# Moving the side work of the eight-head attention phases to other steps

## The chip, the cores and the metric

The kernel runs on one core of a Trainium2 chip. The metric is device time in microseconds (us): the median of three executions, 1615.72 us, with 1610.88 the lowest and 1616.22 the highest. One more execution was profiled; all rows come from it.

## What is computed

Four layers on x of shape (4, 256, 32, 32), float32. Layers 0 and 1 are attention with one head (batch norm, or group norm before it) and aren't touched. Layers 2 and 3 are group norm and attention with 8 heads of 32 channels over 1024 tokens:

```
xn     = groupnorm(x) * w + b                      # 32 groups
q, k, v = split per head of (qkv_w @ xn + qkv_b)
weight = softmax over s of (q_t . k_s) / sqrt(32)  # 1024 x 1024 per head
out    = x_or_xn + proj_w @ (weight @ v) + proj_b  # layer 2 adds xn, layer 3 adds x
```

## The kernel before, in words

The two eight-head layers are computed batch by batch, in groups of four heads: 2 layers x 4 batches x 2 groups = 16 phases, numbered 0 to 15. Every engine runs the same sequence of phases from its own list, and semaphores join them (`all_phases`, L906).

A phase P has 64 steps (`STEPS`). Step s belongs to block J = s // 4 (one tile of 128 keys), head s % 4; steps 0 to 31 are the first half of the queries (h = 0), 32 to 63 the second. In a step TensorE does one score matmul into one of three score banks (L1101) and ScalarE takes its exponential into PR, a ring of four blocks (L1287). Beside this run:

- the weighting of V by the exponentials, eight pieces of one block per half, always two together, at the steps of `WEIGH` (L895); it is TensorE work into psO (L992). `at + 32 * h` is the step; a step past 63 falls into the next phase. Piece 0 of a half waits until VectorE has taken the half before out of psO (`out_done`).
- the sums of the exponentials. GpSimd adds blocks 0 to 5 of a half into PA, five additions (L1328); TensorE multiplies PA and blocks 6 and 7 by ones: the unit "z" (`sums`, L996). VectorE then inverts the sums and scales psO: `take_half` (L1128). The exponentials of a block wait until the ring's slot has been weighted, added or summed: blocks 2 and 10 wait for the sum's reading of block 6, blocks 3 and 11 for the whole z, the others for a weighting and an addition.
- units, TensorE work into one of four banks of psD, in turn, each freed by the engine that takes it; a unit waits until the one four places before it has been taken (`all_taken`, L1012). "a", "m", "e" are 64 tiles of a pass that finds the maxima of the scores, taken by VectorE (L1070, L1152), one per step; "t" and "T" transpose these maxima (L1075), which VectorE negates and SP copies by DMA into a row of the query stacks (L1371) before the next half's scores. "K" and "Q" (two halves each) project the keys and queries of the group after next, taken by ScalarE (L1247, then their rounded "high" part, L1235); GpSimd forms the low part (L1312) and SP copies both into the stacks by 16 DMAs (L1354). "v" are the four value units of the next batch's norm, "p" the four output projections, added to X by VectorE (L1143), "z" the sums.

Odd phases 1 to 13 have K, Q and z only and use `SIDE_AT[0]` (called short here). Even phases 2 to 14 also have v and p and prepare the norm of the next batch (long; `SIDE_AT[1]`). Phase 0 is like a long one without p and with one z, with more tiles (84); phase 15 has no K, Q and only 20 tiles, with p at `LAST_AT`.

The norm in long phases and in phase 0: VectorE's statistics at `BN_AT` (L1189), GpSimd's squares after its third addition and the factors after its fifth (`norm_factors_of`, L115), ScalarE's four passes over the batch at `XN_AT` (two into XH at L1221, two into the unrounded copy at L1223), GpSimd's XL, the rest of it (L1306), in its queue between the additions of the two halves. The first K of a long phase waits for XL (L1040 to L1041). In the short phase, ScalarE waits before it takes the first K until the stack DMAs have read what it will overwrite (L1244 to L1245).

The numbers of a unit are steps: TensorE issues a unit in the first step s with `at <= s`, after that step's score, and the weightings after the units:

```
while todo and todo[0][0] <= s:
    next_unit()
for j, at in WEIGH:
    ...
        if at + HALF_STEPS * h == s:
            weigh(P, p, h, j, place, r)
```

VectorE takes its units and statistics sorted by these same numbers. ScalarE takes a unit one step later, after that step's exponential. GpSimd and SP have no steps: they go through their work in program order as semaphores allow.

Of the kernel before, what the change touches and what calls it, by code (L numbers as in the profile page):

```python
# [38 lines left out]
def attention_stack(nc, x, w0, w1, w2, w3, wp1, wp2, wp3, wv1, par_d, ident_d, gmat_d, out):  # L39
    with ExitStack() as ctx:  # L40
# [51 lines left out]
        def wait(e, s, value):  # L92

            if not isinstance(value, int) or value > 0:
                e.wait_ge(s, value)
# [35 lines left out]
        def single_heads():  # L131

            with ExitStack() as stage:
# [662 lines left out]
                def stack_copies(slot, sides):  # L796
# [17 lines left out]
        LAG = 3  # L814
        ROWS = QUADH * NT // 2

        XN_AT = (31, 34, 35, 36)
        BN_AT = (7.5, 10.5, 15.5, 16.5)

        SIDE_AT = [{"K": (23, 25), "Q": (37.5, 39.5)},  # L820
                   {"v": (6.8, 7.4, 21, 22.5), "K": (47, 49), "Q": (55, 57.5), "p": (15, 39, 16, 23.5)}]
        Z_AT = (37, 6)
        FIRST_AT = {"k": (0.1, 0.2), "q": (0.3, 0.4), "b": (1,), "K": (28.1, 30.1), "Q": (32.1, 34.1)}
        W3_AT = 28
        LAST_AT = {"p": (43.5, 47.5)}
# [4 lines left out]
        def side_units(g, first=False, last=False):  # L830
# [8 lines left out]
            else:  # L839
                halves, step = dict(LAST_AT if last else SIDE_AT[g]), STEPS / max(len(tiles), 4 * ROWS)  # L840
                halves["z"] = Z_AT
                if first:
# [49 lines left out]

        WEIGH = [(0, 10), (1, 10), (2, 19), (3, 19), (4, 28), (5, 28), (6, 33), (7, 33)]  # L895
        PIECES = NT - 1

        def weighed(P, J):
# [30 lines left out]
        def eight_heads_in(stage):  # L929
# [48 lines left out]
            with nc.Block() as block:  # L978
                @block.tensor
                def _(e):  # L980
# [103 lines left out]
                    def phase(P, p, G, g, place, r, layers, proj=None, norm=None, norm_b=None):  # L1084
                        todo = [(at, k) for k, (_, at, _) in enumerate(UNITS[place])]

                        def next_unit():
                            unit(place, r, todo.pop(0)[1], P, p, G, g, norm, layers)
# [7 lines left out]
                        for s in range(STEPS):  # L1096
# [7 lines left out]
# [3 lines that stand above are left out]
                                if at + HALF_STEPS - STEPS == s and not (isinstance(P, int) and P == 0):  # L1107
# [5 lines left out]
                    def tail():  # L1113
                        for j, at in WEIGH:
                            if at + HALF_STEPS >= STEPS:
                                weigh(NGRP - 1, 1, 1, j)
                        e.wait_ge(vec_free, TAIL["vector"] + AFTER - BANKS + 1)
                        sums(bank(4, AFTER), NGRP - 1, 1, LAST_ADDS).then_inc(d_full, 1)
                        for c in range(CT):
                            e.wait_ge(vec_free, TAIL["vector"] + AFTER + c - BANKS + 2)  # L1120
                            output(bank(4, AFTER + 1 + c), 2 * c + 1, 2 * NGRP, 3).then_inc(d_full, 1)
# [5 lines left out]
                def _(e):  # L1127
# [46 lines left out]
                    def phase(P, p, G, g, place, r, layers, proj=None, norm=None, norm_b=None):  # L1174
                        events = [(at, 0, k, "unit") for k, (u, at, i) in enumerate(UNITS[place])
                                  if u not in "vkqKQ"]
                        if norm is not None and P is not None:
                            events += [(at, 0, k, "stats") for k, at in enumerate(BN_AT)]
                        if P is None:
# [27 lines left out]
                def _(e):  # L1207
                    def input_ready(place, r, G, norm, layers):
                        e.wait_ge(factors_done, norm + 1)
                        if place:  # L1210
                            used = [x[::2] for x in UNITS[place]].index(("v", NT // 2 - 1)) + 1
                            e.wait_ge(d_full, base_of("all", place, r) + used)
                            if layers[2] == 3:
                                stacks_filled(e, G)
# [35 lines left out]
                    def phase(P, p, G, g, place, r, layers, proj=None, norm=None, norm_b=None):  # L1250
# [9 lines left out]
                        if norm is not None and P is not None:  # L1260
                            events += [(at, 0, "x", i) for i, at in enumerate(XN_AT)]
                        if layers[0] != layers[1]:
# [7 lines left out]
                        for s in range(STEPS):  # L1270
                            J = s // QUADH
                            if s % QUADH == 0:
# [9 lines left out]
                                else:  # L1282
                                    wait(e, sum_done, ADDS * 2 * P - max(ADDS - 4 - J, 0))
                            if norm is not None and s == XN_AT[0]:
                                input_ready(place, r, G, norm, layers)
# [176 lines left out]
```

## Time and profile before

| | |
|---|---|
| median of three executions | 1615.72 us |
| the profiled execution's own time | 1611.06 us |
| its span | 1609.3 us |
| mean granted TensorE clock | 0.977 of full |
| TensorE, weight loads, VectorE, ScalarE, GpSimd busy | 96%, 61%, 65%, 54%, 61% |
| the 16 eight-head phases | from 549.4 us to the end |

A timeline row reads: start in us from the span's start, duration, engine, line, operation, what it writes from what it reads, shapes, and xN for N merged instructions; in brackets the engine's idle time before it and what ended that. Matmuls are pipelined: a row's duration is longer than the distance to the next start, so distances between starts tell what the engine can do. A row by windows gives, for a stretch, the length, each engine's busy time with the number of instructions of the row's form, the granted clock as a share of full, the share of DMA time and GB/s.

### The profile page before, as it was taken

What the parts mean: (1) busy time and instruction counts of PE and PEld (TensorE: products, weight loads), DVE (VectorE), ACT (ScalarE), POOL (GpSimd) and SP (SyncE); (2) the same over time, 40 slices, a digit from 0 to 9 for tenths busy, and PEclk for the clock granted to TensorE, in tenths of its full rate; (3) what the DMA queues carried; (4) which work ended last, traced back from release to release, by engine and by line L of the source; (5) the groups of instructions that cost most, each with busy time, mean ns of one, the idle gap of its engine ahead of it and who ended that gap; (6) DMA issues with size and microseconds to landing.
All of it is one profiled execution on the core that took longest, in us unless ns stands there. A gap on an engine that the chain in (4) does not pass through costs nothing.

```text
span 1609.3 us, 21730 instructions
## 1 busy us (share of the span) xinstructions
PE 1538.1 (96%) x8246; PEld 987.4 (61%) x8246; DVE 1039.3 (65%) x1658; ACT 866.3 (54%) x1440; POOL 974.5 (61%) x388
## 2 busy tenths in 40 slices
PE   5899979999999899999999999999999999999998
PEld 2777868888887555555555556555555556555542
DVE  3666655454553677777776776777777677777651
ACT  3544414343433366656657657656665665756663
POOL 1222302221213288788798698977878879869883
PEclk7999989999999799999999999999999999999999
DMA  5000000000001503031230330303303123042000
GB/s 190 1 20 20 1 1 1 0 1 0 20 1 40 118 14 79 1 79 34 46 79 1 79 72 28 79 12 69 80 1 80 30 76 79 1 106 65 15 27 27
DMA packets 36392, 67.53 MB, mean 42 GB/s; under 512 B 5760, under 2 KB 7872, under 8 KB 36288
## 3 DMA queue, kind: packets, MB, share of 16 engines
q1 hardware_dynamic: 36144, 65.74, 16.9%
q8 instruction: 66, 1.08, 0.3%
q10 hardware_dynamic: 144, 0.39, 0.1%
q14 instruction: 38, 0.31, 0.1%
HBM read 8.15 MB, written 4.19 MB: 8 GB/s over the span
## 4 chain that ended last, share of the span: by engine, by line
PE 60%; POOL 3%; DVE 3%; issue 1%; SPq 1%; ACT 1%; DMA 0%; DVEq 0%; ACTq 0%; POOLq 0%
PE psO L992 14%; PE psD L1070 13%; PE psD L89 12%; PE psA L1101 10%; PE psD L1004 5%; PE psO L1101 5%; POOL PA L1328 3%; DVE BNS L1152 1%; PE psD L1065 1%; SPq L1362 0%; DVE sums_turned L1131 0%; ACT PR L1287 0%; DVE A L1135 0%; DVE A L1137 0%; POOL KQ L1312 0%
## 5 line engine op out<-in xcount | busy, mean ns | idle before, releaser
L1152 DVE TENSOR_REDUCE BNS<-psD 128x1 f32<-128x512 f32 x1024 | 638.6, 681 | 207.1 <-PE psD L1070 201.7
L1328 POOL TENSOR_TENSOR PA<-PA,PR 128x2048 f32<-128x2048 f32 x126 | 578.5, 4592 | 33.4 <-ACT PR L1287 18.6
L1287 ACT ACTIVATE PR<-psA 128x512 f32<-128x512 f32 x688 | 392.3, 603 | 226.2 <-PE psA L1101 203.4
L1070 PE MATMUL psD<-STK 96*128 96x512 f32 x1016 | 409.0, 407 | 3.8 <-ACT KQ L1247 1.9
L1101 PE MATMUL psA<-STK 97*128 97x512 f32 x688 | 290.1, 424 | 3.9 <-DMA STK<-MROW 2.3
L1287 ACT ACTIVATE PR<-psO 128x512 f32<-128x512 f32 x336 | 202.3, 602 | 159.8 <-PE psO L1101 159.6
L705 POOL TENSOR_SCALAR P<-P,RS 128x1024 f32<-128x1024 f32 x64 | 72.0, 1125 | 330.6 <-DVE RS L413 330.6
L992 PE MATMUL psO<-PR,V 128*32 128x512 f32 x2048 | 246.6, 598 | 5.8 <-DVE A L1137 5.6
L1070 PEld LDWEIGHTS psD<-STK 96*128 96x128 f32 x1016 | 195.5, 193 | 56.1 <-DVE BNS L1152 15.9
L1328 POOL TENSOR_TENSOR PA<-PR 128x2048 f32<-128x2048 f32 x32 | 146.8, 4587 | 99.9 <-ACT PR L1287 99.9
L1101 PEld LDWEIGHTS psA<-STK 97*128 97x128 f32 x688 | 130.4, 190 | 111.1 <-issue 58.0
L1101 PE MATMUL psO<-STK 97*128 97x512 f32 x336 | 146.8, 437 | 1.7 <-DMA STK<-MROW 1.1
L992 PEld LDWEIGHTS psO<-PR,V 128*32 128x32 f32 x2048 | 53.2, 109 | 127.4 <-issue 81.4
L645 ACT ACTIVATE PTH<-psA 128x1024 fp32r<-128x1024 f32 x64 | 65.5, 1024 | 105.0 <-PE psA L301 105.0
L1101 PEld LDWEIGHTS psO<-STK 97*128 97x128 f32 x336 | 63.7, 190 | 84.1 <-issue 46.3
L638 ACT ACTIVATE P<-psD,NM 128x1024 f32<-128x1024 f32 x64 | 71.2, 1113 | 79.3 <-DVE NM L406 78.9
L406 DVE TENSOR_REDUCE NM<-psD 128x1 f32<-128x1024 f32 x64 | 77.8, 1217 | 55.2 <-PE psD L89 54.9
L419 DVE TENSOR_TENSOR PTL<-psA,PTH 128x1024 fp32r<-128x1024 f32 x64 | 78.2, 1221 | 44.9 <-ACT PTH L645 44.9
L316 PE MATMUL psO<-PTH,VH 128*128 128x512 f32 x256 | 105.1, 411 | 0.0
L1312 POOL TENSOR_TENSOR KQ<-KQ 128x1024 fp32r<-128x1024 f32 x32 | 75.8, 2392 | 42.4 <-ACT KQ L1235 42.4
L316 PE MATMUL psO<-PTH,VL 128*128 128x512 f32 x256 | 100.4, 392 | 0.0
L316 PE MATMUL psO<-PTL,VH 128*128 128x512 f32 x256 | 100.0, 391 | 0.0
(159 smaller groups left out, 1951.8 us busy)
## 6 DMA issues: line engine op xcount, KB each, us to landing
STK<-KQ SPq DMA_DIRECT2D x128, 256.0 KB, 3.8
STK<-KQ SPq DMA_DIRECT2D x128, 128.0 KB, 3.7
X<-x SPq DMA_DIRECT2D x4, 1024.0 KB, 7.3
out<-X SPq DMA_DIRECT2D x3, 1024.0 KB, 6.4
XN<-w SPq DMA_DIRECT2D x2, 768.0 KB, 6.5
KH<-KL SPq DMA_DIRECT2D x8, 128.0 KB, 2.8
QH<-KL SPq DMA_DIRECT2D x6, 128.0 KB, 2.4
KQ<-w SPq DMA_DIRECT2D x1, 768.0 KB, 4.3
```

Of the source, the lines that this page charges most:

```text
L89: last = e.matmul(out_ap, w, m, start=(i == 0), stop=(i == len(terms) - 1))
L316: mm = e.matmul(psO[:, t, :], vv[:, s, cols], pp[:, h, s, :], start=(s == k == 0), stop=(s == NT - 1 and k == 2))
L406: e.tensor_reduce(NM[:, g % 4:g % 4 + 1], psD[:, index[u] % 2, :], AX.X, ALU.max, negate=True).then_inc(max_done, 1)
L419: e.tensor_tensor(PTL[:, i // 4, :, cols], psT.rearrange("p (s t) -> p s t", s=NT), PTH[:, i // 4, :, cols].bitcast(F32), ALU.subtract).th ...
L992: mm = e.matmul(psO[cols, 0, :], V[:, j, PART * p + CH * q:PART * p + CH * q + CH], source[:, q, :], start=(j == 0), stop=(j == NT - 1))
L1004: mm = e.matmul(full[CH * q:CH * q + CH, :], ones[:, 0:CH], source[:, q, :], start=(j == NT), stop=(j == NT - 1))
L1070: mm = e.matmul(full, QS[0:STACK, group, int(u in "ae"), q, tile * PART:(tile + 1) * PART], KS[0:STACK, group, h, q, :], start=True, stop= ...
L1101: e.matmul(score_bank(s, p), KS[0:STACK + 1, p, j // (NT // 2), q, j % (NT // 2) * PART:(j % (NT // 2) + 1) * PART], QS[0:STACK + 1, p, h, ...
L1152: top = e.tensor_reduce(MXH[:, h, q, tile:tile + 1], full, AX.X, ALU.max)
L1287: e.activation(PR[:, J % 4, (s % QUADH) * HALF:(s % QUADH + 1) * HALF], score_bank(s, p), ACT.Exp, scale=scale).then_inc(exp_done, 1)
L1312: e.tensor_tensor(low_part(which).bitcast(F32R), low_part(which), high_part(which), ALU.subtract).then_inc(low_done, 1)
L1328: e.tensor_tensor(PA[:, :], PR[:, (J - 1) % 4, :] if j == 1 else PA[:, :], PR[:, J % 4, :], ALU.add).then_inc(sum_done, 1)
```

## The change

Only the step numbers move; no instruction is added or removed, and GpSimd's and SP's programs are as before.

```diff
-        XN_AT = (31, 34, 35, 36)
-        BN_AT = (7.5, 10.5, 15.5, 16.5)
-
-        SIDE_AT = [{"K": (23, 25), "Q": (37.5, 39.5)},
-                   {"v": (6.8, 7.4, 21, 22.5), "K": (47, 49), "Q": (55, 57.5), "p": (15, 39, 16, 23.5)}]
-        Z_AT = (37, 6)
+        XN_AT = (32, 37, 38, 38)
+        BN_AT = (3.5, 12.5, 14.5, 15.5)
+
+        SIDE_AT = [{"K": (25.9, 41.7), "Q": (42.6, 58.2)},
+                   {"v": (9.1, 10.6, 11.9, 24.9), "K": (42.4, 44.5), "Q": (45.5, 50.8), "p": (25.2, 17.2, 26.4, 39.6)}]
+        Z_AT = (41.0, 9.0)
...
-        WEIGH = [(0, 10), (1, 10), (2, 19), (3, 19), (4, 28), (5, 28), (6, 33), (7, 33)]
+        WEIGH = [(0, 15), (1, 15), (2, 21), (3, 21), (4, 29), (5, 29), (6, 35), (7, 35)]
```

`Z_AT` holds the step of z for the first half of the own phase ("z0", 37 to 41) and for the second half of the phase before ("z1", 6 to 9).

## Rows read from the trace of the kernel before

**Rows 1.** The page, busy time and share of each engine:

```profile
PE 1538.1 (96%) x8246; PEld 987.4 (61%) x8246; DVE 1039.3 (65%) x1658; ACT 866.3 (54%) x1440; POOL 974.5 (61%) x388
```

**Rows 2.** Busy time by windows: phases 0, 7, 9, 10 and 15:

```profile
core 0: us, PE busy (x) PEld busy (x) DVE busy (x) ACT busy (x) POOL busy (x), PEclk, DMA share, GB/s
549.43:619.74 70.31, 66.51 (x354) 40.35 (x355) 51.76 (x89) 44.82 (x78) 54.49 (x23) 0.98 0.21 46
...
1012.10:1072.61 60.51, 58.64 (x332) 32.30 (x330) 45.02 (x77) 37.85 (x72) 49.13 (x12) 1.00 0.24 53
...
1144.22:1203.37 59.15, 58.40 (x332) 32.39 (x330) 45.01 (x77) 37.85 (x72) 45.78 (x12) 1.00 0.24 54
1203.37:1274.96 71.59, 71.47 (x398) 41.98 (x399) 50.48 (x88) 44.69 (x78) 62.34 (x26) 1.00 0.20 45
```

**Rows 3.** Timeline of TensorE, the last tiles of phase 9, first score of 10:

```profile
1202.42 0.40 PE L1070 MATMUL psD<-STK 96*128 96x512 f32 x1
...
1202.88 0.39 PE L1070 MATMUL psD<-STK 96*128 96x512 f32 x1
1203.37 0.47 PE L1101 MATMUL psA<-STK 97*128 97x512 f32 x1
```

**Rows 4.** Timeline of TensorE in phase 9: z1, what follows, weighting 0/1:

```profile
1149.63 1.06 PE L1004 MATMUL psD<-PA,ones 128*32 128x512 f32 x8
...
1152.35 0.50 PE L1101 MATMUL psO<-STK 97*128 97x512 f32 x1
1152.69 0.40 PE L1070 MATMUL psD<-STK 96*128 96x512 f32 x1
...
1155.15 1.92 PE L992 MATMUL psO<-PR,V 128*32 128x512 f32 x16 [0.66 <-DVE A L1137]
```

**Rows 5.** Timeline of VectorE behind the same z1:

```profile
1152.48 0.72 DVE L1131 STREAM_TRANSPOSE sums_turned<-psD 128x512 f32<-128x512 f32 x1 [1.54 <-PE psD L1004]
...
1155.01 2.48 DVE L1152 TENSOR_REDUCE BNS<-psD 128x1 f32<-128x512 f32 x4
```

**Rows 6.** Timeline of TensorE in phase 0: score 32, fifth tile behind z0:

```profile
583.01 0.50 PE L1101 MATMUL psO<-STK 97*128 97x512 f32 x1 [1.13 <-DMA STK<-MROW]
...
595.02 0.50 PE L1070 MATMUL psD<-STK 96*128 96x512 f32 x1 [1.35 <-DVE BNS L1152]
```

**Rows 7.** Timeline of ScalarE in phase 10: norm passes two to four:

```profile
1245.10 1.23 ACT L1223 ACTIVATE KQ<-X,SC 128x1024 f32<-128x1024 f32 x1
...
1246.70 1.24 ACT L1221 ACTIVATE XH<-X,SC 128x1024 fp32r<-128x1024 f32 x1
...
1248.31 1.24 ACT L1223 ACTIVATE KQ<-X,SC 128x1024 f32<-128x1024 f32 x1
```

**Rows 8.** Timeline of GpSimd in phase 10: the second XL:

```profile
1249.70 2.37 POOL L1306 TENSOR_TENSOR XL<-KQ,XH 128x1024 fp32r<-128x1024 f32 x1 [0.84 <-ACT KQ L1223]
```

**Rows 9.** Timeline of TensorE in phase 10: an output unit:

```profile
1249.90 1.88 PE L89 MATMUL psD<-A,WP 128*128 128x512 f32 x4
```

**Rows 10.** Timeline of GpSimd: additions of a second half, phases 9 and 10:

```profile
1184.84 4.60 POOL L1328 TENSOR_TENSOR PA<-PR 128x2048 f32<-128x2048 f32 x1 [7.77 <-ACT PR L1287]
...
1256.76 18.85 POOL L1328 TENSOR_TENSOR PA<-PA,PR 128x2048 f32<-128x2048 f32 x4
```

**Rows 11.** Timeline of ScalarE in phase 7: taking the first K:

```profile
1037.87 0.69 ACT L1247 ACTIVATE KQ<-psD,PAR 128x512 f32<-128x512 f32 x1 [1.99 <-DMA STK<-KQ]
```

**Rows 12.** Timeline of TensorE in phase 7, behind that:

```profile
1038.61 0.50 PE L1070 MATMUL psD<-STK 96*128 96x512 f32 x1 [1.11 <-ACT KQ L1247]
```

**Rows 13.** Timeline of TensorE in phase 15: z0:

```profile
1569.31 1.07 PE L1004 MATMUL psD<-PA,ones 128*32 128x512 f32 x8 [2.18 <-POOL PA L1328]
1570.17 3.24 PE L1004 MATMUL psD<-PR,ones 128*32 128x512 f32 x16
```

**Rows 14.** Timeline of GpSimd in phase 15: its first addition:

```profile
1545.78 4.57 POOL L1328 TENSOR_TENSOR PA<-PR 128x2048 f32<-128x2048 f32 x1 [4.04 <-ACT PR L1287]
```

**Rows 15.** Busy time by windows in phase 15, columns as in rows 2:

```profile
1572.00:1574.00 2.00, 2.00 (x10) 0.57 (x3) 0.55 (x1) 0.00 (x0) 0.00 (x0) 0.50 0.00 0
```

## The prediction

> **What bounds the kernel now.** I read the page's busy shares first. TensorE shows 96% [rows 1], but matmuls overlap, so the share alone proves nothing. I then cut the span into its 16 eight-head phases [rows 2]. Phases 1, 3, ... 13 (short) take 59.1 us, phases 2, 4, ... 14 (long, with values, output and the next batch's norm) 71.6 us, each kind the same to 0.1 us, but for phase 7 with 60.5. A phase has 64 steps; a step is one score matmul, one maxima tile and whatever the lists place there.
>
> Next the timeline of TensorE, by starts. A tile follows the last tile after 0.46 to 0.47 us [rows 3], two instructions with no wait between. A sum ("z") holds the stream from 1149.63 to 1152.35, 2.72 us [rows 4]. I added such start-to-start costs over both lists of units: about 57.7 us for a short phase, 70.7 for a long one. So TensorE's own stream is the bound, and true waits are some 1.4 us of a short phase and 0.9 of a long one. The change removes no instruction: all it can win is these waits, 7 x (1.4 + 0.9) = 16 us, and those of phases 0, 7 and 15. What it can lose is new waits at the new places.
>
> The short phase's waits: block 0 of the weighting (step 10) needs the half of the output that VectorE frees after z1; TensorE idles 0.66 us before it [rows 4], 0.73 with the restart. The first score of the next phase comes 0.49 us after the last tile, where 0.24 is usual, as the row of maxima lands late [rows 3]. Some 0.4 us lie behind the two transposes of maxima. In the long phase z1 waits about 0.2 us for GpSimd's last addition; the rest is crumbs.
>
> **The change, part by part.** All in us of one phase.
>
> *z1 from step 6 to 9, weighting 0/1 from 10 to 15 (short phases, and 15).* VectorE starts on a sum 2.85 after the sum's first matmul (1152.48 - 1149.63) and begins its next maxima reduction 5.38 after it; reductions end every 0.6, the first 0.68 after its start [rows 4, 5]. So the first tile behind a sum is read 6.06 to 6.11 after the sum began. Units share four PSUM banks in turn. Before, four tiles (steps 7 to 10) stand between sum and weighting; now six do (10 to 15). The fifth needs the bank of the first: it would be issued 3.06 + 4 x 0.47 = 4.94 after the sum's start [rows 4] and may at 6.11, a wait of 1.17; the next tile loses 0.1 more. This wait is in the trace already: in phase 0, where five tiles follow z0, the fifth idles 1.35 us for the reduction [rows 6]. The weighting then comes later than the 5.5 it needs [rows 4] and waits no more. So 0.73 is removed and 1.27 put in its place: +0.54. Bounds: -0.73 if the banks come free in time, +1.1 if one more reduction stands before; I take the value that rows 6 are nearest to.
>
> The Trainium skill, "Perfetto Trace Analysis", section Optimization Strategy, says that a gap repeating on the engine that should be saturated can mean too little PSUM for the next tile. By it the sign here is a loss, where the removed wait alone would make -0.73 x 8 = -5.8; the trace's 1.35 us agrees with the page.
>
> *Row of maxima, transposes.* The second transpose keeps step 54, but a query unit and both later weightings now lie behind it, 7.7 before the phase's end instead of 6.6, so the 0.24 at the border goes [rows 3]; no key or query stands right behind a transpose any more, -0.2. On SP's queue nothing new stands before that row. Short phase in sum: +0.54 - 0.24 - 0.2 = +0.1; seven give **+0.7** (bounds -6 to +4).
>
> *Long phases.* z1 at step 9 finds GpSimd done: -0.2. Behind z1 three value units separate the tiles, so the bank wait does not come. z0 moves from 37 to 41 with keys and queries at 43 to 46 behind it; the second key half needs the bank of the first tile and loses some 0.25. Crumbs behind transposes and before weighting 8 go, -0.45. Output units and batch-norm statistics (VectorE, steps 3.5 to 15.5) cost the same elsewhere: VectorE is free behind the value units. Sum -0.4; seven give **-2.8** (bounds -5.6 to +3.5).
>
> *Keys five steps sooner, norm passes later.* The first key unit waits on GpSimd's low parts XL. ScalarE's four passes go to steps 32, 37, 38, 38. A pass starts 1.6 after the last when an exponential stands between, at most its own 1.24 when none does [rows 7]; GpSimd's second XL starts 0.15 after the last pass and takes 2.37 [rows 7, 8]. From score 37 that is 0.46 + 0.5 + 1.6 + 2 x 1.24 + 0.15 + 2.37 = 7.55. TensorE comes to the key after 6 x 0.47, an output unit of about 1.75 (four matmuls, 1.88 with their tail [rows 9]), a sum with its restart 2.9 and a score 0.23: 7.7. Cost zero, with a margin of 0.15 only. Bounds 0 and 2 per long phase. In phase 0 no output unit stands between: +1.2 there.
>
> *GpSimd and SP behind it.* Five additions take 4.60 + 18.85 [rows 10]. In the short phase z0 now comes before both queries and one key half, so the second chain starts 36.7 into the phase, not 40.6 [rows 10]; in the long one it starts 0.6 later, behind XL, and ends 1.8 us into the next phase, before exponential 4 asks for it at 4.4. Two low parts and the 16 stack transfers on SP follow; the keys' eviction in the short phase waits for these, and itself moves from step 24 to 27. In phase 7 that wait is 1.99 us on ScalarE [rows 11] and 1.11 on TensorE [rows 12]; three steps later, with a weighting behind it, it is covered: **-1.4** (60.5 - 59.1; bounds -1.4 to 0).
>
> *Exponentials.* Blocks 2 and 10 reuse a buffer that the sum must have read: step 8 now waits for z1 at 9, step 40 for z0 at 41. About 2 us on ScalarE, hidden since no score needs those exponentials until the sum is over (three score banks). If that cover failed it would cost 2 per half.
>
> *Phase 15.* No maxima tiles after step 20; GpSimd's additions end the waits: z0 idles 2.18 us [rows 13], and the granted clock is 0.50 of full behind it, the lower of its levels [rows 15]. GpSimd's chain starts 9.35 into the phase [rows 14], now about 0.95 after z1's start at 6.8, 1.6 sooner; and z0 at 41 lets steps 38 to 41 run first. About 3.3 saved, +0.54 as above: **-2.8** (bounds -4.5 to 0).
>
> *Phase 0.* Score 32 waits 1.13 us for its row of maxima [rows 6]; a weighting now lies between: gone. The 1.35 shrinks to 0.25. Query 0 no longer blocks a bank near its end (-1). Against that the key's +1.2, and some 0.8 more in longer runs of tiles. Net **-1.5** (bounds -4 to +2).
>
> Sum: +0.7 - 2.8 - 1.4 - 2.8 - 1.5 = **-7.8 us**, against the profiled execution's own 1611.06 (span 1609.3): 1603.3. The three runs shown are 1610.88, 1615.72 and 1616.22; with the profiled one they lie at two levels 5 us apart, so the same sum on the median 1615.72 is 1607.9. I state the middle, **1606**. A measurement of this kernel can tell about 0.3%, 5 us, from no change.
>
> **Rivals.** Times from 1611.06.
> 1. *Nothing measurable.* New waits eat the gain: the bank wait is 1.8 instead of 1.27 in eight phases (+4.2) and phase 0 wins nothing (+1.5): -2.1 in all, 1609. For: three of the gains are read from one phase each. Against: rows 6 fix the bank wait's size. Chance 0.20.
> 2. *Slower.* The key unit of the long phases waits on XL. Place: step 43, behind ScalarE's norm passes; margin 0.15. It decides from 1.8 us late: 7 x 1.8 = 12.6 turns -7.8 into +4.8. At 2.5 late it is +9.7, 1621. For: if exponential 37 lags, the passes and XL lag with it. Against: exponential 37 follows a weighting, where ScalarE has just caught up. Chance 0.08.
> 3. *The clock falls* behind the new 1.2 us idle. Sixteen matmuls of a sum take 3.24 us at the lower level [rows 13], at full clock some 2.72 x 16/24 = 1.8 [rows 4]: 1.4 x 7 = 10 lost, +2, 1613, no change. Against: short phases keep 1.00 with an idle of 0.66, and phase 0, with its 1.35, has 0.98 over all [rows 2]. Chance 0.04.
>
> A page speaks for rival 3: the Trainium skill, "TensorE: Matmul & The Clock Gate", section A second HAM failure mode: psum-queue depth-cycling, where small idles between groups that cycle through banks let the clock swing. The trace has the fall in phase 15 alone.
>
> **How the numbers follow.** The forecast has 0.68, the rivals 0.20, 0.08 and 0.04. The range 1596 to 1616 holds the forecast at both levels, part of the better bounds (-13 on the lower level) and rival 1. Faster by over 0.3%: 0.68; within: 0.20 + 0.04 = 0.24; slower: 0.08.
>
> **What would show it.** Right: short phases at 59.0 to 59.4 us with an idle of 1.1 to 1.3 us at the tile of step 14, released by VectorE, and none before weighting 0; long phases near 71.2 with the key at 43 unhindered; phase 7 no longer apart; phase 15 near 70. Wrong: an idle before the key units released by GpSimd; short phases under 58.5 (no bank wait) or over 60; a granted clock under 1.00 in short phases.

## The result and the profile after

The changed kernel takes 1618.15 us (median of 15 executions, 1614.22 to 1620.25), the kernel before 1613.5 beside it (15 executions, 1610.88 to 1617.14): a ratio on record of 1.0031 (the two medians alone give 1.0029), 95% interval 1.0022 to 1.0039. It is slower by 0.3%, 4.65 us, and 2.15 us above the top of the forecast range. The two profiled executions, spans 1617.7 and 1609.3, differ by 8.4. Of that, 1.6 lie ahead of the eight-head stage, in code that the change does not touch; over thirteen profiled kernels that code took between 546.8 and 551.7 us, so these 1.6 are not the change's. Another 1.7 are the clock's at the very end of phase 15, which came out differently in these two profiles (last section); 5.1 are left, near the 4.65 of the medians. The 6.8 us of the eight-head stage, these 1.7 included, have their places:

| us | before | after | difference | forecast |
|---|---|---|---|---|
| phase 0 | 70.31 | 67.58 | -2.7 | -1.5 |
| phases 1, 3, 5, 9, 11, 13, each (phase 3 after: 60.09) | 59.15 | 59.86 | +0.7 | +0.1 |
| phase 7 | 60.51 | 59.85 | -0.7 | -1.3 |
| phases 2, 4, 8, 10, 12, 14, each | 71.61 | 71.45 | -0.15 | -0.4 |
| phase 6 | 71.68 | 76.08 | **+4.4** | -0.4 |
| phase 15 | 72.83 | 75.08 | +2.2 | -2.8 |

Against the forecast of -7.8, these +6.8 are 14.6 too much: phase 15 has 5.0 of them, phase 6 4.8, the seven short phases 4.6, the other long ones 1.4; phase 0 is 1.2 better. The extra 0.2 of phase 3 came back in every profile of the changed lists and was not followed up.

By windows, phases 6 and 15 of the kernel before (columns as in [rows 2]):

```profile
940.42:1012.10 71.68, 71.52 (x398) 41.96 (x399) 50.50 (x88) 46.02 (x80) 62.45 (x27) 1.00 0.23 56
```

```profile
1536.43:1609.26 72.83, 62.00 (x334) 24.69 (x332) 23.88 (x40) 33.63 (x66) 41.81 (x11) 0.97 0.04 15
```

and of the changed kernel, phases 0, 6, 7, 9, 10 and 15:

```profile
550.99:618.58 67.59, 66.28 (x355) 40.38 (x356) 51.89 (x90) 45.24 (x78) 52.61 (x22) 0.97 0.21 48
941.25:1017.33 76.08, 72.86 (x398) 42.99 (x399) 50.79 (x88) 46.35 (x80) 61.62 (x26) 0.98 0.22 53
1017.33:1077.18 59.85, 58.74 (x331) 32.49 (x330) 45.02 (x77) 38.26 (x72) 49.92 (x13) 1.00 0.24 54
1148.63:1208.49 59.86, 58.75 (x331) 32.49 (x330) 45.00 (x77) 38.26 (x72) 51.11 (x13) 1.00 0.24 54
1208.49:1279.94 71.45, 71.45 (x398) 41.79 (x399) 50.62 (x88) 44.99 (x78) 57.09 (x25) 1.00 0.20 45
1542.58:1617.66 75.08, 64.27 (x334) 25.20 (x332) 23.76 (x40) 33.62 (x66) 42.72 (x11) 0.95 0.04 15
```

A phase whose length differs from its like is where to look first: phase 6 stands 4.6 us over phase 10, with the same list of units. Its TensorE timeline stops at step 43:

```profile
990.08 0.50 PE L1101 MATMUL psA<-STK 97*128 97x512 f32 x1
990.41 0.40 PE L1070 MATMUL psD<-STK 96*128 96x512 f32 x1
990.65 0.39 PE L1101 MATMUL psA<-STK 97*128 97x512 f32 x1
994.26 0.70 PE L89 MATMUL psD<-XH,WH 128*128 128x512 f32 x2 [3.22 <-POOL WL L1337]
```

and GpSimd's, in the same stretch:

```profile
976.13 0.20 POOL L129 TENSOR_TENSOR SC<-PAR,TMP 128x2 f32<-128x2 f32 x1
985.61 2.38 POOL L1306 TENSOR_TENSOR XL<-KQ,XH 128x1024 fp32r<-128x1024 f32 x1 [9.27 <-ACT KQ L1223]
988.35 2.38 POOL L1306 TENSOR_TENSOR XL<-KQ,XH 128x1024 fp32r<-128x1024 f32 x1 [0.36 <-ACT KQ L1223]
990.69 3.43 POOL L1337 TENSOR_TENSOR WL<-KQ,WH 128x1536 fp32r<-128x1536 f32 x1
```

Phase 6 is where the weights change from layer 2 to layer 3. The key unit needs the low part of the new weights, WL, which GpSimd takes behind both XL. XL was ready in time (988.35 + 2.38 = 990.73), as forecast; WL ends at 994.12. Before, the key came at step 47, at 994.66, after WL's end at 992.57, and nothing waited:

```profile
989.09 3.48 POOL L1337 TENSOR_TENSOR WL<-KQ,WH 128x1536 fp32r<-128x1536 f32 x1
```

In the short phases, TensorE of phase 9 behind z1 (the rows that answer to [rows 4]):

```profile
1155.45 1.06 PE L1004 MATMUL psD<-PA,ones 128*32 128x512 f32 x8
...
1160.15 0.39 PE L1101 MATMUL psA<-STK 97*128 97x512 f32 x1
1161.57 0.51 PE L1070 MATMUL psD<-STK 96*128 96x512 f32 x1 [1.03 <-DVE BNS L1152]
1161.91 0.40 PE L1101 MATMUL psA<-STK 97*128 97x512 f32 x1
1162.16 0.49 PE L1070 MATMUL psD<-STK 96*128 96x512 f32 x1
1162.59 1.92 PE L992 MATMUL psO<-PR,V 128*32 128x512 f32 x16
```

The fifth tile starts 6.12 after z1 (1161.57 - 1155.45), when VectorE has read the first; the weighting waits no more. Both are the forecast's. The page on which the prediction leaned here, the Trainium skill's "Perfetto Trace Analysis", section Optimization Strategy (a gap that repeats on the engine that should be saturated can mean too little PSUM for the next tile), agrees with this trace: the gap of 1.03 stands in every short phase.

In phase 15, TensorE from z0 on:

```profile
1577.11 1.90 PE L1004 MATMUL psD<-PR,ones 128*32 128x512 f32 x16
1578.94 0.50 PE L1101 MATMUL psA<-STK 97*128 97x512 f32 x1
1579.28 0.40 PE L1101 MATMUL psO<-STK 97*128 97x512 f32 x1
1579.51 0.39 PE L1101 MATMUL psA<-STK 97*128 97x512 f32 x1
1581.80 3.16 PE L89 MATMUL psD<-A,WP 128*128 128x512 f32 x4 [1.90 <-issue]
1583.97 1.42 PE L1101 MATMUL psA<-STK 97*128 97x512 f32 x1
```

TensorE reaches score 42 2.5 us sooner, but the output unit p0, left at 43.5, now has three scores between itself and z0 instead of seven. It needs the half that VectorE takes after z0 (`take_half`), and TensorE idles 1.90. The profile calls this idle "issue" and names no releaser; VectorE's last operation on that half ends at 1581.70, and p0 starts at 1581.80:

```profile
1581.01 0.69 DVE L1137 TENSOR_TENSOR A<-psO,A 128x512 f32<-128x512 f32 x1
```

### The profile page after: what moved, and what is told of

Its sections match the earlier page's. It is cut to its first block, busy times and chain, and to the rows that moved or that the text cites. A ratio compares the mean times of both kernels' runs of the same rounds, so it can differ in the third digit from the quotient of the medians.

```text
span 1617.7 us, 21730 instructions
## 1 busy us (share of the span) xinstructions
PE 1547.0 (96%) x8246; PEld 990.7 (61%) x8246; DVE 1040.1 (64%) x1658; ACT 871.8 (54%) x1440; POOL 974.6 (60%) x388
## 4 chain that ended last, share of the span: by engine, by line
PE 64%; DVE 2%; ACT 1%; issue 1%; POOL 1%; DVEq 0%; DMA 0%; ACTq 0%; POOLq 0%
PE psO L992 15%; PE psD L1070 14%; PE psD L89 12%; PE psA L1101 11%; PE psD L1004 5%; PE psO L1101 5%; PE psD L1065 1%; DVE BNS L1152 1%; DVE sums_turned L1131 0%; DVE A L1135 0%; DVE A L1137 0%; ACT PR L1287 0%; POOL PA L1328 0%; PE psD L1075 0%; POOL WL L1337 0%
## 5 line engine op out<-in xcount | busy, mean ns | idle before, releaser
L1070 PE MATMUL psD<-STK 96*128 96x512 f32 x1016 | 416.3, 415 | 8.7 <-DVE BNS L1152 8.7
L1101 PE MATMUL psO<-STK 97*128 97x512 f32 x336 | 143.4, 427 | 0.9 <-ACT PR L1287 0.8
```

Of the source, the lines that this page charges most:

```text
L1070: mm = e.matmul(full, QS[0:STACK, group, int(u in "ae"), q, tile * PART:(tile + 1) * PART], KS[0:STACK, group, h, q, :], start=True, stop= ...
L1101: e.matmul(score_bank(s, p), KS[0:STACK + 1, p, j // (NT // 2), q, j % (NT // 2) * PART:(j % (NT // 2) + 1) * PART], QS[0:STACK + 1, p, h, ...
```

## The experiments

Each is the changed kernel with one edit, unless said. Lengths of phases repeat to about 0.1 us from run to run (phase 15 excepted). Where only one time is given, it is that of the profiled execution, and the reading goes by the lengths of phases, not by that total.

**Keys and queries of the long phases back.**

```diff
-"K": (42.4, 44.5), "Q": (45.5, 50.8)
+"K": (47, 49), "Q": (55, 57.5)
```

> The changed kernel with the keys and queries of the long phases back at steps 47, 49 and 55, 57.5; all else as changed. Theory A (the early key waits for the split of layer 3's weights, once, in phase 6): phase 6 falls from 76.1 us to 71.4 to 71.8, its first key starts without an idle, the other phases stay within 0.2 us, short ones at 59.85. Rival B (phase 6 is longer because GpSimd's additions and XL come later after the moved sum): phase 6 stays above 74 us. Time about 4.5 us under the changed kernel by A, no change by B.

Measured: one time of 1631.84. Phase 6 took 73.58, as the other long phases: its extra is gone, so it does hang on the key's place. But every long phase went from 71.45 to 73.58, and phase 0 from 67.58 to 71.92. With tiles instead of keys behind z0, the fifth meets the bank again: 1.3 of the 2.1, with the restart. Another 0.6 stands at the weighting at 61; what it waits for was not followed. TensorE in phase 10 of this run:

```profile
1265.45 0.39 PE L1101 MATMUL psA<-STK 97*128 97x512 f32 x1
1266.89 0.50 PE L1070 MATMUL psD<-STK 96*128 96x512 f32 x1 [1.04 <-DVE BNS L1152]
```

So the key's new place pays for much of the sum's: these two moves belong together.

**Phase 15's output units later.**

```diff
-LAST_AT = {"p": (43.5, 47.5)}
+LAST_AT = {"p": (47.5, 51.5)}
```

> The changed kernel with phase 15's two output units four steps later (47.5 and 51.5), so as far behind the moved sum as before; all else as changed. Theory A (the first output unit waits there for VectorE's half of the output, and the TensorE clock falls behind the idle): the idle of 1.90 us is gone, the output unit takes about 1.9 us and not 3.16, and phase 15 up to its last score shortens by 2.5 to 3.5 us from 56.99. Rival B (phase 15 is longer because of its other moved steps, the weighting pieces or GpSimd): less than 1 us.

Measured: 1615.55; phase 15 72.24 instead of 75.08, the rest unchanged. z0 (3.14 and 3.15) and the end behind score 63 (18.09 in both) took the same time in the two profiles, so the 2.84 are p0's: its wait, and the slow matmuls behind the wait. TensorE goes from score 44 to score 45, where p0's wait stood, in 0.62:

```profile
1578.44 0.40 PE L1101 MATMUL psA<-STK 97*128 97x512 f32 x1
1579.06 0.49 PE L1101 MATMUL psA<-STK 97*128 97x512 f32 x1 [0.22 <-ACT PR L1287]
```

**Weighting blocks 0 and 1 sooner, everywhere.**

```diff
-WEIGH = [(0, 15), (1, 15), ...
+WEIGH = [(0, 13), (1, 13), ...
```

> The changed kernel with weighting pieces 0 and 1 at step 13 instead of 15; all else as changed. Theory A (the wait is for a PSUM bank at the fifth tile behind a sum): with four tiles between sum and weighting the tile at step 14 waits no more, the weighting idles 0.6 to 0.9 us for VectorE instead, and short phases fall from 59.85 to 59.1 to 59.4 us. Rival B (VectorE's work behind the sum has to be waited for in any order): the wait of the weighting is as long as the tile's was, 1.3 us, and short phases stay at 59.7 to 60. Long phases within 0.2 us by both.

Measured: 1625.05. The short phases fell to 59.00, as theory A has it, but the long ones rose to 73.24 and phase 0 to 70.98, which neither theory had. There the weighting at 45 no longer covers the time in which ScalarE takes the key and query units; TensorE in phase 10 of this run:

```profile
1270.26 0.51 PE L1070 MATMUL psD<-STK 96*128 96x512 f32 x1 [0.34 <-ACT KQ L1247]
1270.61 0.40 PE L1101 MATMUL psO<-STK 97*128 97x512 f32 x1
1270.85 0.40 PE L1070 MATMUL psD<-STK 96*128 96x512 f32 x1
1271.89 0.50 PE L1101 MATMUL psA<-STK 97*128 97x512 f32 x1 [0.64 <-ACT PR L1287]
```

**These three at once.**

> The three edits together (keys and queries of the long phases back, phase 15's output later, weighting 0/1 at step 13), the rest as changed. By theory A of the three: 4.5 + 3 + 7 x 0.6 = 11 to 12 us under the changed kernel, so about 1606 to 1607 where the changed kernel has 1618, and 6 to 8 us under the kernel before (0.4 to 0.5%). By the rivals: no faster than the kernel before.

Measured: 1621.96 (seven executions) against 1612.63 (twelve), ratio on record 1.0044 (1.0058 by the medians), interval 1.0024 to 1.0063. A miss: phase 6 was cured (73.21), but the long phases stood at 72.80 and phase 0 at 71.79. Repairs that each undo a part of the change for all phases take away its gains too; the next ones touch one phase type each.

**Blocks 0 and 1 sooner in the short phases alone.**

```diff
 for j, at in WEIGH:
+    at -= 2 * (j < 2 and place == 2)
```

> The changed kernel, with blocks 0 and 1 of the weighting at steps 13 and 45 in phases 1, 3, ... 13 alone; the long phases keep 15 and 47. Theory A (the loss of the short phases is the fifth tile's bank, behind a sum, in front of a weighting that came too late; what the run with 13 everywhere lost, it lost in the long phases, where the weighting at 47 covers ScalarE's keys and queries): short phases 58.9 to 59.0 us instead of 59.85, long phases 71.45 as in the changed kernel, phase 6 76.1, phase 15 75.1; the span 6 us below the changed kernel's at equal length before the eight-head phases. Rival B (the 0.9 us of the short phases in that run were paid for by work pushed over the border, so that the long phases lose the 1.8 whatever their own steps are): long phases 73.2 again. Rival C (run to run): short phases at 59.85.

Measured: 1611.12. Short phases 59.00, long 71.52, phase 6 76.15: theory A. In the first half step 13 takes 3.16, with the weighting's old wait in it, as step 10 did before, and steps 14 and 15 wait no more; in the second half step 45 takes 2.42 where step 47 took 2.62.

**The low part of the weights first.**

```diff
 factors(norm, place, r, layers[2])
-input_low(norm, norm_b, layers[2])
 if layers[0] != layers[1]:
     e.wait_ge(w3_high, 1)
     e.tensor_tensor(WL[:, :, :], ...).then_inc(w3_split, 1)
+input_low(norm, norm_b, layers[2])
```

> The changed kernel, with GpSimd taking the low parts of layer 3's weights (3.4 us) before the low parts of the input in phase 6, instead of after them. Theory A (phase 6 lost 4.4 us because its first key unit, now at step 43, waits for the low parts of the weights, which stood in GpSimd's queue behind those of the input; GpSimd idles 9 us ahead of these): phase 6 at 71.4 to 71.8 us instead of 76.08, the key at step 43 with a wait under 0.5 us, every other phase as in the changed kernel. Rival B (ScalarE's rounding of the weights in phase 6 makes the norm passes late, and the split is only what ends last): phase 6 stays over 73, the key waiting for the low parts of the input instead. Rival C (GpSimd's port or memory conflicts with the exponentials' additions): the additions lengthen, phase 6 over 74.

Measured: 1617.19; phase 6 71.53, every other phase but the last within 0.1. GpSimd in phase 6, WL now in the stretch in which it had idled, and TensorE's key behind it:

```profile
978.07 3.50 POOL L1336 TENSOR_TENSOR WL<-KQ,WH 128x1536 fp32r<-128x1536 f32 x1 [1.14 <-ACT WH L1228]
986.24 2.38 POOL L1306 TENSOR_TENSOR XL<-KQ,XH 128x1024 fp32r<-128x1024 f32 x1 [4.67 <-ACT KQ L1223]
988.98 2.38 POOL L1306 TENSOR_TENSOR XL<-KQ,XH 128x1024 fp32r<-128x1024 f32 x1 [0.36 <-ACT KQ L1223]
```

```profile
991.27 0.39 PE L1101 MATMUL psA<-STK 97*128 97x512 f32 x1
991.62 0.70 PE L89 MATMUL psD<-XH,WH 128*128 128x512 f32 x2
```

Theory A again: 4.5 us of the result were this one order. Phase 15 took 76.63 here, for a reason given below.

**The same in the kernel before.**

> The kernel before, with GpSimd's low parts of layer 3's weights taken before those of the input (the repair of phase 6, in the kernel that did not need it). Theory A (before the change the key unit came at step 47, after the split had ended, so the order on GpSimd cost nothing): phase 6 at 71.6 to 71.8 us as before, all phases as before. Rival B (taking the split first is worth something by itself, since the low parts of the input end ScalarE's or GpSimd's queue later or sooner): phase 6 under 71.2 or over 72.2. It is also a second profile of the kernel before's last phase: up to its score 63 56.2 to 56.7 us, and a tail of 16.4 or 18.1 us, as the clock falls there or not.

Measured: 1612.11; phase 6 71.56, as before. Unexpected: phase 7 took 59.18 instead of 60.51, as the other short phases. So the wait of [rows 11] came from this same split. In GpSimd's queue the second chain of additions and then the low parts of keys and queries stand behind it; these low parts end 8.7 us into phase 7 before and 5.3 with the split first (phase 7 starts at 1012.10 and 1012.75), and SP's transfers into the stacks follow them:

```profile
1016.06 4.73 POOL L1312 TENSOR_TENSOR KQ<-KQ 128x1024 fp32r<-128x1024 f32 x2
```

```profile
1013.35 4.74 POOL L1312 TENSOR_TENSOR KQ<-KQ 128x1024 fp32r<-128x1024 f32 x2
```

**Three repairs of one place each**: the short phases' weighting, the split, phase 15's output units.

> The changed kernel with three repairs at once: blocks 0 and 1 of the weighting at 13 and 45 in the short phases alone, GpSimd's low parts of the weights before those of the input, and phase 15's output units at 47.5 and 51.5. Theory A (the change's losses are these three places, and they are independent): minus 6.3 (seven short phases at 58.95), minus 4.5 (phase 6), minus 2.8 (phase 15), together 13.6 us below the changed kernel, about 1604.5 against a median of 1618.15, that is 0.5 to 0.6% below the kernel before. Rival B (they draw on the same slack): half of it or less, no measurable difference from the kernel before. Phases: short 58.95, long 71.45, phase 6 71.6, phase 15 72.3, phase 0 67.6.

Measured: 1603.8 (six executions, 1603.26 to 1606.31) against 1613.21 (eleven executions): ratio 0.9937, interval 0.9918 to 0.9956, faster than the kernel before by 0.6%. Short 58.94, long 71.45, phase 6 71.45, phase 15 72.27, phase 0 67.54, each as expected. That of phase 15 is partly luck: against the run with p0 later, z0 took 4.84 instead of 3.14 and the end behind score 63 16.4 instead of 18.1, which cancel. The total doesn't hang on it: all six executions lie below the eleven of the kernel before. The change's losses are, in the main, these three places.

**Blocks 4 and 5 one step later, in the kernel before.**

```diff
-(4, 28), (5, 28)
+(4, 29), (5, 29)
```

> The kernel before, with blocks 4 and 5 of the weighting one step later (29 and 61 instead of 28 and 60) and nothing else. Theory A (phase 0 of the kernel before lost 1.13 us at score 32 because the row of maxima was late, and any work that stands before that score takes its place): little changes there, since the weighting stays on the same side of the score: phase 0 at 70.0 to 70.4, short phases 59.1 within 0.1, long phases 71.6 within 0.2. Rival B (the one step is what gave phase 0 its gain): phase 0 near 69.2. Either way it tells whether this part of the change carries anything by itself.

Measured: 1615.36; phase 0 70.89, short 59.38, long 72.09: it loses in all phases but 7, which neither theory had. In phase 0 score 32 no longer waits for its row, but the wait reappears at the weighting of step 33. Its second block needs exponential 31, and ScalarE holds that one until GpSimd's factors of the norm are there (idle 2.79 to 582.00, released by L129): the wait for the factors stands before the exponential of the first step in `XN_AT`, which is 31 here. TensorE at that weighting:

```profile
580.24 1.07 PE L992 MATMUL psO<-PR,V 128*32 128x512 f32 x8
582.65 1.07 PE L992 MATMUL psO<-PR,V 128*32 128x512 f32 x8 [1.35 <-ACT PR L1287]
```

So the step alone doesn't bring phase 0's gain. The change also moves the first pass, and with it the wait for the factors, behind exponential 31, and the weighting from 33 to 35; how much each of these gives was not tested apart.

**Two runs on the 0.24 us before the first score of a long phase** [rows 3], which the change left as they were. The first puts a weighting before that score, in the kernel with three repairs:

```diff
+    at += 2 * (j in (4, 5)) * (place == 2) - 2 * (j < 2 and place == 2)
```

> The kernel with the three repairs, and in the short phases blocks 4 and 5 of the weighting at 31 and 63 instead of 29 and 61, so that 1.9 us of matmuls stand between the last tile of a short phase and the first score of the next. Theory A (the first score of a long phase comes 0.24 us late because its score bank is that of score 62, two scores before and not three, and exponential 62 has just ended): the 0.24 goes, short phases 58.7 instead of 58.94; long phases within 0.3 of 71.45. Rival B (the wait is for the row of maxima, whose DMA lands just then): the border keeps whatever is left of it, but the row is written 7 us before, so this gives the same here; the next run tells A from B. Rival C (the weighting at 31 makes the exponentials of block 8 late, which need the ring's slot): short phases longer, 59.2 or more.

Measured: one time of 1609.81. The 0.24 are covered, but the short phases rose to 59.65: the longer run of tiles behind the query half idles 0.40 until ScalarE has taken it, and a step behind the key half takes 0.27 longer. Rival C's size, by another wait. The second run turns the score banks:

```diff
-i = (s + p) % SCORE_BANKS
+i = (s + 2 * p) % SCORE_BANKS
```

with the first number of exponentials that scores 0 and 1 ask for changed to match.

> The changed kernel with the score banks of odd phases turned by one more: bank (s + 2p) mod 3 instead of (s + p) mod 3, and the wait that goes with it. A phase has 64 scores, and two phases 128, which three does not divide, so that one border in two must have a bank that comes back after two scores. Theory A (the 0.24 us at the end of the short phases are that bank): the distance of 0.47 from the last tile to the first score moves from the borders of short to long phases to those of long to short ones, 0.23 stands at the others: short phases 59.6, long phases 71.7, no difference in sum. Rival B (the row of maxima, which my prediction named): the 0.47 stays where it is, short 59.85, long 71.45.

Measured: 1617.07; short 59.69, long 71.69, as theory A has it. TensorE at the end of phase 8 and at the end of phase 9 of this run, last tile and first score:

```profile
1145.54 0.40 PE L1070 MATMUL psD<-STK 96*128 96x512 f32 x1
1146.01 0.47 PE L1101 MATMUL psO<-STK 97*128 97x512 f32 x1
```

```profile
1205.49 0.40 PE L1070 MATMUL psD<-STK 96*128 96x512 f32 x1
1205.72 0.40 PE L1101 MATMUL psA<-STK 97*128 97x512 f32 x1
```

The distance of 0.47 has moved to the end of the long phases. It is the bank: 128 scores in three banks bring one back after two scores instead of three, and score 0 waits for exponential 62.

## Why the prediction was wrong

Its direction failed, by two steps that each missed a wait, and by sizes.

1. *"Cost zero, with a margin of 0.15 only"*, the key five steps sooner. The step that failed: it asked only when XL ends, and then carried the price of phase 10 to all seven long phases. In six of them it held: TensorE has no wait for XL there. The key in phase 6 also waits for WL, in GpSimd's queue behind XL: +4.4 where -0.4 stood. The row of WL was in the trace of before, in one phase alone. Rival 2 (slower, the key waits on GpSimd for XL) had the right place and the wrong operand; its price was 1.8 to 2.5 in seven phases, not 4.4 in one. That 1618 lies near its 1621 is luck.
2. *Phase 15, -2.8.* The forecast held up to score 42, which came at 36.4 us of the phase instead of 38.9. Part of that is the clock's: in four of the ten profiles with z0 at 41, the step of z0 takes 4.8 instead of 3.15 and score 42 comes at 38.0. The failing step: what stands behind a moved sum was priced for the weighting and the tiles, not for p0, whose input is the sum's result. With p0 at its old step the interval from score 44 to 45 is 4.46 instead of 1.55. Up to score 63 the phase is 0.8 slower in these two profiles, and 55.3 to 58.6 us against 56.2 over the six with p0 at 43.5, as the clock falls or not; the wait of 1.90 is in all six. Behind score 63 the table's 2.2 has 1.7 from the clock, below, and -0.25 that was not followed up.
3. *Short phases, +0.1.* The bank wait was right in kind and near in size: the step takes 1.29 more, the next 0.12, for 1.17 and 0.1; and 0.73 went, as said. But the border's -0.24 never came. The step "the row of maxima lands late" read a cause into [rows 3] that the row doesn't name; the run that turns the score banks shows a bank. And the second half, priced at nothing, lost 0.2: at step 47 the tile has the bank of the query half at 43, and ScalarE takes that one at 1192.01, so that the tile starts only behind it (with the weighting at 45 this 0.2 went, as seen above). ScalarE and TensorE in phase 9 of the changed kernel:

```profile
1192.01 0.68 ACT L1247 ACTIVATE KQ<-psD,PAR 128x512 f32<-128x512 f32 x1
```

```profile
1192.74 0.50 PE L1070 MATMUL psD<-STK 96*128 96x512 f32 x1
1193.17 1.93 PE L992 MATMUL psO<-PR,V 128*32 128x512 f32 x16
```

   1.29 + 0.12 + 0.2 - 0.73 - 0.14 (keys no longer behind a transpose) = +0.74, the measured 0.7.
4. *Long phases, -0.4.* z1's wait (-0.2) and the second key half's bank (+0.2) came as priced; of the 0.45 of "crumbs" only about 0.15 went, a term that had no row of its own.
5. *Phase 7, -1.4.* Right in sum: it lost its 1.4 against the other short phases. The cause given, a stack transfer that ScalarE meets later, was only the last link; in the kernel before, the split before XL alone removes it. There the key is taken 23.7 us into the phase without a wait, the low parts having ended at 5.3; in the changed kernel they end at 5.0. So the later step that the forecast named was not needed: its number came right by luck.
6. *Phase 0, -1.5.* It won 2.7. The row wait and the fifth tile's 1.35 went as said; the key's wait was sized 1.2 and is 0.28, in part since the score before z0 itself waits 0.52 for an exponential. These parts of phase 0 are read from the rows; only the row wait was tested by a run. TensorE in phase 0 of the changed kernel:

```profile
590.67 0.50 PE L1101 MATMUL psO<-STK 97*128 97x512 f32 x1 [0.52 <-ACT PR L1287]
...
595.54 0.70 PE L89 MATMUL psD<-XH,WH 128*128 128x512 f32 x2 [0.28 <-POOL XL L1306]
```

7. Rival 3, the clock: it didn't fall in the short phases (1.00 in all of them, with the idle of 1.03). The page named for it, the Trainium skill's "TensorE: Matmul & The Clock Gate", section A second HAM failure mode: psum-queue depth-cycling, tells of small idles between groups that cycle through banks; no run here shows a fall in these phases.

The range was too narrow at its upper end: the long phases' bound was taken for the kind, and phase 6 is not like its kind; phase 15's upper bound was 0, and the wait that it met was in no term.

## What to carry to other kernels

When a unit is moved sooner, list every wait its code has, the conditional ones too, and price each in the phase where it is active: here the exceptional phases (new weights, last) decided, not the typical one. Behind a moved producer, follow everything that reads its result as well as everything that shares its buffers. And a repair is best placed where the loss is: undoing parts of this change for all phases made it slower, three local edits made it 0.6% faster than the kernel before.

## What the runs showed of the hardware

The same idle before the same instructions gives two outcomes. The last output units follow an idle of 2.78 or 2.79 us in all thirteen profiles; the eight matmuls then take 3.67 (three profiles) or 5.31 to 5.37 (ten). Before, changed, and the kernel with three repairs:

```profile
1602.36 3.67 PE L89 MATMUL psD<-A,WP 128*128 128x512 f32 x8 [2.79 <-issue]
```

```profile
1609.05 5.37 PE L89 MATMUL psD<-A,WP 128*128 128x512 f32 x8 [2.79 <-issue]
```

```profile
1595.31 3.67 PE L89 MATMUL psD<-A,WP 128*128 128x512 f32 x8 [2.79 <-issue]
```

In the changed kernel the granted clock is 0.50 of full in the window 1610 to 1612, the lower of its two levels; in the kernel before it is 1.00 from 1602 to 1606. The 5.37 appeared in a profile of the kernel before with one step moved as well (that of blocks 4 and 5), and with the split first. The kernel before and the same with the split first have one list for phase 15, and end it 1.7 us apart; so do the changed kernel with p0 later (5.37) and that with three repairs (3.67). z0 at step 41 takes 3.15 or 4.84 us (score 41 to 42, changed kernel and that with the split first). p0 at 43.5 follows an idle of 1.89 or 1.90 in six profiles, and its four matmuls take 1.95 in two of them and 3.16 to 3.62 in four. Such falls make the 76.63 above, and are why phase 15 is compared here up to its score 63 or between runs with equal ends. Phase 6 showed a fall too, behind its 3.22 us of idle: 0.50 from 996 to 998, so its 4.4 hold the wait and a slow stretch behind it. What decides between the two outcomes after an equal idle stays open.
